# Eight tiles of a decoder kernel moved by 4 to 256 bytes, so that loaded and streamed operands lie at eight distances

## The reference

```
x = layernorm(x + attn(x))     # qkv = x Wqkv^T + b; elu(q)+1, elu(k)+1; running sums of k and k*v over tokens;
                               # y = q * cumsum(k*v) / clip(sum_d q * cumsum(k)); y Wproj^T + b
x = layernorm(x + xattn(x, ctx))  # channel attention, 4 heads of 128 channels, two sets of scales and biases
x = layernorm(x + ffn(x))      # one of 8 experts per sequence (argmax of a router on the token mean):
                               # relu(x W1 + b1) W2 + b2, hidden size 2048
```

## Time and profile before

| | us |
|---|---|
| median of 3 runs | 2460.48 (2459.77 to 2462.58) |
| the profiled execution's own time | 2461.27 |
| its span, first to last instruction | 2459.6 |
| PE busy / PEld busy | 2387.3 / 1977.4 |
| DVE / ACT / POOL busy | 1737.4 / 1148.0 / 560.8 |

### The profile page before, as it was taken

How to read it: one execution, slowest core, us unless ns; L and a number is a source line. 1 busy time by engine, 2 the same in 40 slices (tenths; PEclk the granted TensorE clock), 3 DMA queues, 4 the chain that set the end, 5 groups by cost and what they waited for, 6 DMA issues and landing times.

```text
span 2459.6 us, 33255 instructions
## 1 busy us (share of the span) xinstructions
PE 2387.3 (97%) x11584; PEld 1977.4 (80%) x11584; DVE 1737.4 (71%) x2721; ACT 1148.0 (47%) x1920; POOL 560.8 (23%) x452
## 2 busy tenths in 40 slices
PE   6779999999999999999999999999999999999997
PEld 5558888888888888888888888888888888888786
DVE  6667777686876768677686876768677686876553
ACT  4334445444554454545444544454545544544543
POOL 2231312312132122312312132122312312132210
PEclk9889999999999999999999999999999999999999
DMA  7333425244343433525344343443524334232331
GB/s 275 115 133 122 174 89 185 99 137 159 103 173 106 145 143 120 193 86 180 108 135 161 102 173 108 139 149 120 189 90 174 114 130 167 96 136 91 103 108 68
DMA packets 83400, 331.85 MB, mean 135 GB/s; under 512 B 11810, under 2 KB 11810, under 8 KB 72738
## 3 DMA queue, kind: packets, MB, share of 16 engines
q1 hardware_dynamic: 83234, 329.72, 39.0%
HBM read 306.61 MB, written 23.07 MB: 134 GB/s over the span
## 4 chain that ended last, share of the span: by engine, by line
PE 94%; DVE 2%; ACT 1%; issue 1%; DMA 1%; POOL 1%; ACTq 0%; POOLq 0%; DVEq 0%; SPq 0%
PE acc L1040 28%; PE h_ps L1024 10%; PE h_ps L1026 9%; PE h_ps L1025 9%; PE m L862 7%; PE m L890 7%; PE m L891 7%; PE m L892 7%; PE m L942 2%; PE m L996 2%; PE m L901 2%; PE m L1010 1%; PE m L914 1%; PE m L964 1%; PE m L949 1%
## 5 line engine op out<-in xcount | busy, mean ns | idle before, releaser
L763 DVE TENSOR_TENSOR h_lo<-hid,h_hi 128x512 fp32r<-128x512 f32 x256 | 299.6, 1170 | 266.5 <-ACT h_hi L434 266.0
L429 ACT ACTIVATE hid<-h_ps,b 128x512 f32<-128x512 f32 x256 | 176.4, 689 | 605.9 <-PE h_ps L1026 605.1
L1024 PE MATMUL h_ps<-x2T_hi,we_hi 128*128 128x512 f32 x1024 | 412.4, 403 | 1.7 <-DVE x2T_lo L749 1.3
L1040 PE MATMUL acc<-we_hi,h_hi 128*128 128x512 f32 x1024 | 413.1, 403 | 0.0
L1026 PE MATMUL h_ps<-x2T_hi,we_lo 128*128 128x512 f32 x1024 | 399.6, 390 | 0.0
L1040 PE MATMUL acc<-we_hi,h_lo 128*128 128x512 f32 x1024 | 399.3, 390 | 0.0
L1040 PE MATMUL acc<-we_lo,h_hi 128*128 128x512 f32 x1024 | 399.1, 390 | 0.0
L1025 PE MATMUL h_ps<-x2T_lo,we_hi 128*128 128x512 f32 x1024 | 398.9, 390 | 0.0
L376 ACT ACTIVATE e_f<-m,sb_qkv,scale 128x512 f32<-128x512 f32 x128 | 99.7, 779 | 550.2 <-PE m L892 550.2
L755 DVE TENSOR_TENSOR we_lo<-raw,we_hi 128x1024 fp32r<-128x1024 f32 x256 | 326.9, 1277 | 23.0 <-ACT we_hi L419 22.8
L890 PE MATMUL m<-xT_hi,wq 128*128 128x512 f32 x768 | 304.9, 397 | 17.6 <-DVE wq L545 11.4
(11 more groups left out here) (128 smaller groups left out, 3739.1 us busy)
## 6 DMA issues: line engine op xcount, KB each, us to landing
raw<-in_w SPq DMA_DIRECT2D x256, 512.0 KB, 3.9
wq<-wq_scratch SPq DMA_DIRECT2D x180, 512.0 KB, 3.3
xT_raw<-in_xT SPq DMA_DIRECT2D x16, 1024.0 KB, 4.8
x<-in_x_tok SPq DMA_DIRECT2D x16, 1024.0 KB, 5.5
ctx_T<-in_ctxT SPq DMA_DIRECT2D x16, 1024.0 KB, 8.2
ctx_tok<-in_ctx_tok SPq DMA_DIRECT2D x16, 1024.0 KB, 6.3
out_dram<-x SPq DMA_DIRECT2D x16, 1024.0 KB, 4.8
wq_scratch<-wq SPq DMA_DIRECT2D x12, 512.0 KB, 4.1
```

Source lines behind the costliest of these rows:

```text
L429: act.activation(hid[:, f % 2, :], H_PS[:, :], ACT.Relu, bias=b1[:, b % 2, f:f + 1]).then_inc(h_done, 1)
L763: dve.tensor_tensor(h_lo[:, f % 2, :], hid[:, f % 2, :], h_hi[:, f % 2, :].bitcast(F32), ALU.subtract).then_inc(hlo_done, 1)
L1024: pe.matmul(H_PS[:, :], we_hi[:, g % NW, js], x2T_hi[:, j, :], start=(j == 0), stop=False)
L1040: last = pe.matmul(acc[t][:, :], hx[:, f % 2, ts], wx[:, g % NW, C:], start=(f == 0 and n == 0), stop=(f == FC - 1 and n == 2))
```

## The change

A helper `moved(name, n, by)` allocates a tile of `n * 512 + 128` elements a partition, 512 bytes more than before, and returns a view that begins `by` elements (4 * `by` bytes) behind the tile's start. Eight tiles are made with it. Their sizes stay multiples of 512 bytes, so all other tiles keep their place within 512 bytes, and the whole takes 4 KiB more a partition. No instruction is added, removed or moved on any engine: the order of each engine's instructions is the same row for row, and only the addresses of some operands differ.

```diff
+        def moved(name, n, by):
+            tile = sb(name, [P, n * 512 + 128], F32R)
+            return tile[:, by:by + n * 512].rearrange("p (n e) -> p n e", n=n)
+
...
-        wp_hi, wp_lo = sb("wp_hi", [P, CC, C], F32R), sb("wp_lo", [P, CC, C], F32R)
+        wp_hi, wp_lo = moved("wp_hi", CC, 14), moved("wp_lo", CC, 48)
...
-        xT_hi, xT_lo = sb("xT_hi", [P, CC, T], F32R), sb("xT_lo", [P, CC, T], F32R)
+        xT_hi, xT_lo = moved("xT_hi", CC, 16), moved("xT_lo", CC, 64)
         y_hi, y_lo = xT_hi, xT_lo
-        x2T_hi, x2T_lo = sb("x2T_hi", [P, CC, T], F32R), sb("x2T_lo", [P, CC, T], F32R)
-        h_hi, h_lo = sb("h_hi", [P, 2, T], F32R), sb("h_lo", [P, 2, T], F32R)
+        x2T_hi, x2T_lo = moved("x2T_hi", CC, 2), moved("x2T_lo", CC, 4)
+        h_hi, h_lo = moved("h_hi", 2, 1), moved("h_lo", 2, 8)
```

## The result

| | before | after |
|---|---|---|
| median of 4 runs, us | 2460.96 (2459.77 to 2462.58) | 2498.35 (2495.48 to 2499.60) |
| ratio | | 1.015, 95% interval 1.0138 to 1.0162 |
| span of the profiled execution, us | 2459.6 | 2495.7 |

The changed kernel is 37.4 us slower. I had forecast no change, 2461 us, with 0.24 on slower. The time came out on the upper edge of the range of 2420 to 2498 us. That is luck: the upper part of the range was there for rival B (2489 us), and rival C (2501 us), which comes nearest to what happened, was given 0.08 and left outside it.

A forecast was written before the change was run, and what follows sets the result against it. TensorE's own queue, at 0.2267 us a product, was taken as the bound. The sum 2461.27 + 0 + 0.5 + 0 = 2461.8 us, 2461.0 against the median, gave 2461 us; range 2420 to 2498, no change itself 2456 to 2466.

The forecast's parts named there:

- rival B: In down, h_hi's 4-byte offset doubles the excess of each load, 27.3 us more, 2489 us; chance 0.16, or a part.
- rival C: All fp32r products: equal offsets are the best case, shifted operands settle at 0.231 us, 40 us more, 2501 us; chance 0.08.
- Part 1: Distance between streamed and loaded operand in all 9216 products: taken as 0, between bounds of -122.9 and +122.9 us.
- rival A: TensorE's products: the 13.3 ns excess is a collision of places that shifting ends, down to 2338 us; chance 0.23.
- Part 2: Operands off 16-, 32- or 64-byte marks span one piece more, 0.42 ns each: 0 to 2 us, 0.5 in the sum.
- Part 3: Writing and reading the moved tiles on ScalarE and VectorE: same durations expected, nothing charged, TensorE still the bound.

The follow-up runs named there:

- the sweeps: Decoder left out, TensorE alone runs blocks of 60 products at set distances; the second adds finer steps, smaller loads, shorter streams, bf16; 226.7 ns a product at distance 0.
- e4_h_back: The changed kernel with h_hi and h_lo put back to 0, the other six tiles still moved; 2488.63 us, ratio 1.0115 to the kernel before.
- e7_all16: The kernel before with all operands of fp32r products moved together by 16 bytes, every distance still 0; 2504.72 us, ratio 1.0179.

## Why the prediction was wrong in its main term

Part 1, the distance, is the step that failed. I took 0 between the bounds of -122.9 and +122.9 us, because load and stream would walk past each other through all residues, so that the distance could only say where they meet. It measured +37.8 us by the paces. In the sweeps single distances other than multiples of 256 cost from 2.2 (12, 28, 60, 64 and 320 bytes) to 13.3 ns (20 and 68 bytes), so how often they meet does hang on it, if meeting it is. The bounds held; the value in them was chosen by an argument that no row carried.

What I had read and under-used is the earlier trace rows: behind the transposes the pace was 0.231 us for ten steps. Those rows end before the return to 0.2267 that I stated; the rows under e4_h_back show it. I used it for rival A and put C, which rests on it, at 0.08, since "no offset in bytes has a reason to undo" the return to 0.2267. The offsets do undo it. At equal places on marks of 32 bytes there is one steady relation of load and stream; at others the steps go round in a cycle (at 64 bytes, in ns, 226, 229, 232 and again), with a mean of 229 to 240. C's price, 4.3 ns x 9216 = 40 us, was right within 3 us, in part by luck: the four kinds of product lost between 3.0 and 5.3 ns, and their mean, 4.1, happens to lie near what the disturbed steps lose. C is right in its number and in "equal offsets are the best case", for streams of 512 columns and full loads; it was wrong in speaking of one other pace.

Rival A fell: no distance gave less than 226.7 ns at 512 columns, in 22 blocks at places equal modulo 256 bytes (226.6 or 226.7), in 46 random patterns, or at any step of the two sweeps. Rival B fell as the cause: `h` alone is 13.9 us and not 27.3, and multiples of 64 cost too.

Part 2 (0.42 ns for each 16-byte piece crossed, 1.9 us) failed as well: both operands moved by 16 bytes cross no more pieces of 16 bytes than before and lose 3.3 to 6.7 ns a product. The Trainium skill's rule of 16-byte lines (SBUF — State Buffer, "Specifications (TRN2)"), which would have left all multiples of 16 harmless, does not describe this. The Trainium skill's rule of two independent read ports (TensorE: Matmul & The Clock Gate, "Step-by-step: what each phase is for") fits the bf16 blocks, 215.8 ns at both distances that were run. It does not account for those of fp32r: with the stream left at 0 and only the load moved by 64 bytes, the pace goes from 226.7 to 233.3.

Part 3 held: the elementwise durations on the moved tiles are within 8 ns of before, VectorE at 108.6 us a period, no new wait.

The cause is shown as far as this: it is TensorE's pace at full clock; it hangs on the places of the fp32r operands, of loads and of streams, modulo 256 and against marks of 32 bytes, and on the order in which places follow each other; it needs nothing from other engines or DMA, since the sweeps run without them. What in the chip does it is open. That the load takes read turns from the stream in proportion to its size is excluded by the loads of 32 columns, which made products slower; a fixed cost plus something that depends on how a product's reads fall against the one before would fit, but that is only argued.

## What to carry to other kernels

Keep all operands of full fp32r products (128x128 loaded, 512 columns streamed) at places that agree modulo 256 bytes and are multiples of 32, in all kinds of product that follow each other: here that is worth 1.5% to 1.8% of the kernel (the changed kernel and e7_all16), and small tiles or padding allocated ahead of the large ones can lose it unseen. When a steady pace is disturbed in a trace and comes back, the pace in between hints at what losing that state costs: here it was 4.3 ns a product, and the kinds of product lost 3.0 to 5.3. Where a term's bounds are wide and the row nearest to it shows another value than 0, take the row.

## What the runs showed that I had not expected

- fp32r products of one layout can have more than one steady pace, 230.0 and 233.3 ns with both operands moved by 16 bytes, by how the run of products began; in the decoder 231.1 is a third.
- Two distances in turn can be dearer than either: 64 bytes alone gives 228.9 ns, 256 alone 226.7, and the pattern 64, 256, 64 gives 233.3.
- None of it shows at half clock: `qkv` takes 426.4 ns a product before and 426.7 after.
- Loading 32 columns instead of 128 made the products slower, 231.7 against 226.7 ns.
- A single product in ten at another place costs the ten up to 4.3 ns each.
